# Expert regions over the whole layer, and a reordered preparation, in a macaron block with a routed mixture

## The chip, the cores and the metric

The kernel runs on one core of one Trainium2 chip. The metric is the device time of one execution in microseconds (us); the profiled execution is a run of its own. Engines: PE (TensorE, matrix products; PEld its weight loads), DVE (VectorE), ACT (ScalarE), POOL (GpSimd), SP (SyncE, which here only issues DMAs); "SPq" is an engine's sequencer.

## The reference

x is 2 x 2048 tokens of 256 numbers. Three residual steps follow one another: half a mixture of experts, a linear attention, and half the same mixture again.

```python
def _L0_ffn_ref(h, router_w, rn_g, rn_b, w1, ln_g, ln_b, w2, on_g, on_b):   # 4 experts, hidden 512
    h_norm = layer_norm(h, rn_g, rn_b)
    g = softmax(einsum('bsd,ed->bse', h_norm, router_w))
    top2_w, top2_idx = top_k(g, 2)
    top2_w = top2_w / (sum(top2_w) + EPS_GATE)
    hid = relu(layer_norm(einsum('bsd,edh->bseh', h, w1), ln_g, ln_b))
    expert_out = einsum('bseh,ehd->bsed', hid, w2)
    out = sum(take_along_axis(expert_out, top2_idx) * top2_w)
    return layer_norm(out, on_g, on_b)
x = x + 0.5 * _L0_ffn_ref(_layernorm(x), ...)
x = x + _L0_attn_ref(_layernorm(x), ...)     # Z = cumsum(v k^T), y = q Z, 16 heads of 16
x = x + 0.5 * _L0_ffn_ref(_layernorm(x), ...)
```

## The kernel before

**Tiles.** The 4096 tokens are 32 token tiles of 128 (`NT`); 16 of them make a group (`GT`), 8 an octet (`TO`), 4 a quad (`TB`). A mixture takes the groups G = 0, 1 (first mixture, f = 0) and 2, 3 (second, f = 1). For each group the tokens are routed: normalised (`quad_norm`, `quad_rstd`, `quad_factors`, `quad_again`), written as two f16 parts (`row` on ACT, `row_low` on DVE), turned (`row_T`), multiplied by the router (`router`), and for each octet `logits`, `exps`, `choose`, `prefix` and `place` find the two experts of every token and its row in an expert's region of the DRAM tensor `slots_in`. POOL's `scatter` then writes each token tile twice (two indirect DMAs). Each region is closed by rows of zeros (`pads`, SP). `tables` works out, from the counts, which expert (`etab`) and which row (`rtab`) each *slot tile* of 256 rows belongs to. With 4 experts, a group's 4096 slots fill at most `NJ` = 16 + 3 = 19 slot tiles, so a mixture runs `NP` = 38, the kernel 76.

**A slot tile.** SP loads its rows (`load_slots`: two transposing DMAs into `hT`, one plain into `hs`; 5 buffers of `hT`, 3 of `hs`) up to `AHEAD` = 5 slot tiles ahead. On PE: `grams` (variance of the hidden row by the Gram matrix of w1), `std_T`, `layer1` in two halves, `layer2` of the slot tile before in two halves. DVE: `twice_low`, `variances`, `std_parts`, `relu_low`; POOL: `pair_std` (the power -1/2 of the variance, L613); ACT: `std_row`, `relu_high`, `scale_out`. SP stores the scaled result (`store_slots`) to `slots_out`. PE runs `grams` two slot tiles ahead, so slot tile j + 2's load has to have landed when slot tile j begins.

**Order.** Each engine's queue is written out by hand in a function `mixture(f)` of its own; an engine does its queue in order, and semaphores are the only links. SP's queue at slot tile p is: store p - 1, then load p + 5. At the first load of a group (J = 0) it first writes that group's pads and waits until all 16 token tiles of the group are scattered and `tables` is done; whatever stands behind it in SP's queue, stores included, waits too.

**Beside the slot tiles** of a mixture's first group (J = 0 to 18) the second group is routed: `ROUTED` spreads the 16 token tiles over J = 0 to 9, `OCTET_AT` = (5, 10) says where an octet's logits stand, `moves` where POOL scatters it: two token tiles each at J = 7 to 10 and 12 to 15. `tables` stands at J = 12. At J = 14 to 17 DVE adds an offset to X, and in the first mixture `ahead` scales the attention's weights there (`attention_maxima`, `max_row(3)`, `attention_scales`). Beside the second group's slot tiles (from J = 1 on) the first group's results are gathered, weighted and normalised, one token tile per slot tile (`gather`, `first_weighted`, `token_sum`, `token_out`). The second group's results leave during the attention (f = 0) or at the end (`gather_last`, f = 1).

**Preparation**, before the first slot tile, in the `weights` functions: the first group is routed whole, w1 is centred (`centre`), turned (`w1_T`) and multiplied into 4 Gram matrices (`w1_gram`, 16 f32 matmuls each; Gram e waits for `gram_low(e - 2)` on DVE), the scale of w1 is found (`hidden_scales`), gamma is multiplied in (`with_gamma`), w1 is cut in two f16 parts (`w1_high`, `w1_low`), the scale of w2 is found (`output_scale`) and w2 is cut too (`w2_high`, `w2_low`). `layer2` reads w2's parts; in the second mixture they are loaded back from `w2_kept`, since the attention keeps rows in their place.

## Time and profile before

| | us |
|---|---|
| median of 3 runs (1130.91 to 1135.23) | 1131.0 |
| the profiled execution, whole | 1138.73 |
| its span, first to last instruction | 1137.0 |

In the profiled execution the first `layer1` matmul (L1893) starts at 133.8 us; slot tiles 0 to 37 (first mixture) run to about 426, the attention to about 786, slot tiles 38 to 75 to 1072, and the rest gathers and normalises the last group. Slot tile j of the second mixture is number 38 + j. A slot tile has 8 matmuls of line L1893, which makes that line a clock for the others.

### The profile page before, as it was taken

The numbers are of one execution on the slowest core, as the hardware profiler recorded it, in microseconds if no ns is written. First come the engines' busy times: TensorE is split into PE (matmuls) and PEld (weight loads), VectorE is DVE, ScalarE is ACT, GpSimd is POOL, SyncE is SP. The second block draws the span as 40 slices with busy tenths as digits, with TensorE's granted clock in tenths as the row PEclk, the third lists the DMA queues.
The fourth block names the chain that finished last, engine by engine and source line by source line (L and its number), as shares of the span: only waits on it lengthen the run. The fifth ranks groups of instructions, "written<-read, shape, count | busy, mean of one in ns | idle before, by whom it ended". The sixth has DMA issues, their size and how long they took to land.

```text
span 1137.0 us, 26666 instructions
## 1 busy us (share of the span) xinstructions
PE 872.4 (77%) x8596; PEld 662.4 (58%) x8596; DVE 732.4 (64%) x2104; ACT 500.6 (44%) x958; POOL 561.3 (49%) x631
## 2 busy tenths in 40 slices
PE   1543499978999897798788787775799989999700
PEld 1432387856888774565555554443687778888500
DVE  4547776666777754598787764372675774878335
ACT  2642366422444454565565555430565333444311
POOL 4146224551456453687685366354226542555373
PEclk9956599999999998999899899995899999999955
DMA  8042654563566411111121112123645657666343
GB/s 296 10 158 111 157 155 127 152 168 106 130 158 163 130 63 24 40 40 46 43 51 46 23 44 68 31 77 107 159 103 158 155 154 155 163 159 151 118 131 107
DMA packets 191146, 126.06 MB, mean 111 GB/s; under 512 B 126373, under 2 KB 180905, under 8 KB 190633
## 3 DMA queue, kind: packets, MB, share of 16 engines
q1 hardware_dynamic: 177746, 89.72, 30.1%
q0 software_dynamic: 12288, 33.57, 10.1%
q8 instruction: 79, 1.29, 0.5%
q10 hardware_dynamic: 984, 1.07, 0.3%
q14 instruction: 49, 0.40, 0.1%
HBM read 50.89 MB, written 47.19 MB: 86 GB/s over the span
## 4 chain that ended last, share of the span: by engine, by line
PE 48%; DVE 14%; issue 13%; POOL 7%; ACT 6%; DMA 5%; SPq 3%; another core or an unknown queue 3%; ACTq 0%; DVEq 0%; POOLq 0%
PE banks L1908 4%; PE banks L1895 4%; PE banks L1893 4%; PE banks L1894 4%; PE banks L1910 4%; PE banks L1909 4%; PE banks L1993 4%; POOL slots_in L605 3%; PE banks L1995 3%; PE banks L2106 3%; PE banks L1994 3%; PE banks L1869 2%; PE banks L1870 2%; DMA area<-slots_out,pos 2%
## 5 line engine op out<-in xcount | busy, mean ns | idle before, releaser
L613 POOL TENSOR_TENSOR stds<-vare,expo 128x4 f32<-128x4 f32 x76 | 80.5, 1059 | 208.3 <-DVE vare L920 207.0
L1908 PE MATMUL banks<-w2all,area 128*128 x608 | 167.0, 275 | 6.3 <-DMA w2all<-w_kept 3.6
L1893 PE MATMUL banks<-area,w1h 128*128 128x256 f16 x608 | 169.1, 278 | 2.1 <-DVE area L934 1.9
L1895 PE MATMUL banks<-area,w1l 128*128 128x256 f16 x608 | 168.5, 277 | 0.9 <-issue 0.9
L1894 PE MATMUL banks<-area,w1h 128*128 128x256 f16 x608 | 168.9, 278 | 0.3 <-issue 0.2
L1910 PE MATMUL banks<-w2all,area 128*128 x608 | 166.7, 274 | 1.8 <-issue 1.8
L1909 PE MATMUL banks<-w2all,area 128*128 x608 | 166.7, 274 | 0.0
L934 DVE SCALAR_TENSOR_TENSOR area<-banks,area 128x512 f16<-128x512 f32 x152 | 104.4, 687 | 88.2 <-ACT area L1451 75.2
L1451 ACT ACTIVATE area<-banks 128x512 f16<-128x512 f32 x152 | 89.6, 590 | 123.8 <-PE banks L1895 99.8
L605 POOL DMA_INDIRECT slots_in<-area,spos x96 | 102.9, 1072 | 75.4 <-DVE spos L855 49.6
L737 POOL TENSOR_TENSOR area<-area 128x512 f16<-128x512 f32 x64 | 79.3, 1244 | 119.0 <-ACT area L1663 118.4
L1459 ACT ACTIVATE area<-banks,stds 128x256 f32<-128x256 f32 x152 | 70.9, 466 | 98.6 <-PE banks L1910 80.3
L629 POOL DMA_INDIRECT area<-slots_out,pos x96 | 97.0, 1010 | 25.8 <-issue 21.6
L1993 PE MATMUL banks<-area 64*128 64x32 f16 (+1 forms) x766 | 76.6, 226 | 41.5 <-issue 21.5
L1869 PE MATMUL banks<-gramh,area 128*128 x304 | 77.9, 290 | 24.9 <-issue 11.0
L1993 PEld LDWEIGHTS banks<-area 64*128 64x128 f16 (+1 forms) x766 | 39.9, 96 | 77.7 <-issue 51.0
L915 DVE CUSTOM_DVE_ANT_0 area<-banks,area 128x256 f16<-128x256 f32 x152 | 58.3, 420 | 33.0 <-PE banks L1870 27.2
L1995 PE MATMUL banks<-area 64*128 64x32 f16 (+1 forms) x766 | 75.9, 221 | 4.5 <-issue 4.5
L1870 PE MATMUL banks<-graml,area 128*128 x304 | 77.9, 291 | 0.6 <-issue 0.6
L1994 PE MATMUL banks<-area 64*128 64x32 f16 (+1 forms) x766 | 75.5, 222 | 2.2 <-issue 2.2
L1663 ACT ACTIVATE area<-area 128x512 f16<-128x512 f32 x64 | 40.1, 628 | 71.1 <-DVE area L1325 68.4
L1908 PEld LDWEIGHTS banks<-w2all,area 128*128 128x128 f16 x608 | 59.5, 98 | 19.5 <-issue 7.5
(278 smaller groups left out, 2226.3 us busy)
## 6 DMA issues: line engine op xcount, KB each, us to landing
area<-slots_in SPq DMA_DIRECT2D x76, 256.0 KB
slots_out<-area SPq DMA_DIRECT2D x152, 128.0 KB
X<-in_L_attn_x_dram SPq DMA_DIRECT2D x8, 512.0 KB, 6.1
slots_in<-zrow SPq DMA_DIRECT2D x16, 256.0 KB
area<-area SPq DMA_DIRECT2D x256, 16.0 KB
out_dram<-X SPq DMA_DIRECT2D x32, 128.0 KB
area<-slots_in SPq DMA_TRANSPOSE x152
area<-in_L_ffn_w_dram SPq DMA_DIRECT2D x4, 512.0 KB, 11.7
```

Source lines behind the costliest of these rows:

```text
L605: pool.indirect_dma_start(slots_in[G % 2], bass.IndirectOffsetOnAxis(spos[:, O % 2, k, j:j + 1], 0), rows_of(i).rearrange("p c d -> p (c d ...
L934: dve.scalar_tensor_tensor(out=Rl[:, p % 2, ms].rearrange("p m t -> p (m t)"), in0=bank[k][:, :], scalar=0.0, in1=Rh[:, p % 2, ms].rearran ...
L1869: pe.matmul(o, a[:, c], gramh[c][:, bass.ds(e, 1), :], start=(c == 0), stop=False)
L1893: pe.matmul(o, w1h[c][m][:, bass.ds(e, 1), :], a[:, c], start=(c == 0), stop=False)
L1894: pe.matmul(o, w1h[c][m][:, bass.ds(e, 1), :], a[:, KC + c], start=False, stop=False)
L1895: last = pe.matmul(o, w1l[c][m][:, bass.ds(e, 1), :], a[:, c], start=False, stop=(c == KC - 1))
L1908: pe.matmul(o, Rh[:, p % 2, k, rows], w2h[k][:, bass.ds(e, 1), :], start=(k == 0), stop=False)
L1909: pe.matmul(o, Rh[:, p % 2, k, rows], w2l[k][:, bass.ds(e, 1), :], start=False, stop=False)
L1910: last = pe.matmul(o, Rl[:, p % 2, k, rows], w2h[k][:, bass.ds(e, 1), :], start=False, stop=(k == HC - 1))
L1993: pe.matmul(o, lh, rh, start=start, stop=False, **kw)
L1994: pe.matmul(o, lh, rl, start=False, stop=False, **kw)
L1995: return pe.matmul(o, ll, rh, start=False, stop=stop, **kw)
```

## The change

1. An expert's region now holds a whole mixture, 32 token tiles, and the counts run on over both groups (`carry` isn't cleared between them). So a mixture's slot tiles are `NP` = 32 + 3 = 35, and the kernel's 70. `slots_in` and `slots_out` are one tensor each.
2. As not all tokens are routed when the first slot tiles run, `tables` is done in three phases (`PHASE` = 0, 5, 13): slot tiles 0 to 4 need octet 0 alone, 5 to 12 the whole first group, 13 to 34 everything. SP waits for octets and table at slot tiles 0, 5 and 13. `positions` has to map a row through these segments. Its rows are longer than before.
3. The second group is routed sooner: token tiles over j = -1 to 4, logits at j = 2 and 5, POOL's scatters 3, 3 and 2 token tiles at j = 4, 5, 6 and again at 7, 8, 9; pads at j = 9, the last table at j = 8. Loads of slot tiles 13 and up are issued 4 ahead, and none before j = 10 (`load_at`). The first group leaves from j = 20 on by `LEFT`, one or two token tiles per slot tile, 13 slot tiles in all.
4. In the preparation the Grams stand sooner in the queues of PE, ACT and DVE, the first table right behind octet 0, both quads' statistics of the next group before the first slot tile, and w2's low parts behind the first slot tiles' variances. The last 4 token tiles of the first group are scattered between POOL's first `pair_std`. `std_T(p + 1)` now stands ahead of `layer1(p)` on PE.
5. In the attention two tables are worked out (phases 0 and 1 of the second mixture) instead of one, and SP's first five loads of the second mixture wait for octet 0 alone; the reload of w2 waits for both octets.

The diff, cut to its core:

```diff
-    REG = GT * P + S2
+    NO = NT // TO
+    NP = NT + E - 1
+    SPARE = NT * P + S2
+    REG = SPARE + (E - 1) * S2
+    PHASE = (0, TO - E + 1, GT - E + 1, NP)
+    SEGS = (1, 3, 4)
+    NB = SEGS[-1] * E
+    K1 = GT + E - 1
     AHEAD = 5
...
+
+        ROUTED = (0, 3, 6, 8, 11, 14, 16)
+        OCTET_AT = (2, 5)
+        MOVED = (3, 3, 2)
+        LEFT = (2, 1, 1, 2, 1, 1, 2, 1, 1, 1, 1, 1, 1)
+        LAST_AT = 10
         OFFSET_AT = 14
 
+
+        def started(j):
+            return ROUTED[max(0, min(j + 2, len(ROUTED) - 1))]
+
         def routed(j):
-            return tuple(range(ROUTED[j], ROUTED[j + 1])) if j + 1 < len(ROUTED) else ()
+            return range(started(j - 1), started(j))
 
 
         def moves(j):
             for o, at in enumerate(OCTET_AT):
-                if at + 2 <= j < at + 2 + TO // 2:
-                    t = TO * o + 2 * (j - at - 2)
-                    return t, t + 1
+                k = j - at - 2
+                if 0 <= k < len(MOVED):
+                    return range(TO * o + sum(MOVED[:k]), TO * o + sum(MOVED[:k + 1]))
             return ()
...
+        def leaves(j):
+            k = j - K1 - 1
+            return range(sum(LEFT[:k]), sum(LEFT[:k + 1])) if 0 <= k < len(LEFT) else ()
+
...
             def load_slots(p):
-                G, J = group(p)
-                if J == 0:
-                    pads(G)
+                f, j = p // NP, p % NP
+                if j in PHASE:
+                    sp.wait_ge(r_tab, 3 * f + PHASE.index(j) + 1)
+                if j == PHASE[0]:
+                    sp.wait_ge(sc_h[0], 32 * TO * (2 * f + 1))
+                if j == PHASE[1]:
+                    sp.wait_ge(sc_h[1], 32 * TO * (2 * f + 1))
+                if j == PHASE[2]:
                     for o in range(GO):
-                        sp.wait_ge(sc_h[o], 32 * TO * (G + 1))
-                    sp.wait_ge(sc_p[G % 2], 16 * E * (G // 2 + 1))
-                    sp.wait_ge(r_tab, G + 1)
-                row = sp.value_load(rtab[0:1, G % 2, J:J + 1], min_val=0, max_val=(E - 1) * REG + GT * P - S2)
+                        sp.wait_ge(sc_h[o], 32 * TO * (2 * f + 2))
+                    sp.wait_ge(sc_p, 16 * E * (f + 1) + 16)
+                row = sp.value_load(rtab[0:1, j:j + 1], min_val=0, max_val=E * REG - S2)
                 wait(sp, b_A, 2 * (p - R_HT + 1))
                 for k in range(2):
...
+            def load_at(j):
+                return j - AHEAD if j < PHASE[2] else max(j - AHEAD, LAST_AT, j - 4)
...
+                    for o in range(GO):
+                        sp.wait_ge(sc_h[o], 32 * TO * 3)
                     sp.wait_ge(m_w2, 16)
                     sp.dma_start(w2flat, w2_kept).then_inc(m_w2, 16)
-                for p in range(p0, p1):
-                    if p > p0:
-                        store_slots(p - 1, 0)
-                        store_slots(p - 1, 1)
-                    if p + AHEAD < p1:
-                        load_slots(p + AHEAD)
-                store_slots(p1 - 1, 0)
-                store_slots(p1 - 1, 1)
+                for j in range(NP):
+                    if j > 0:
+                        store_slots(p0 + j - 1)
+                    if j == LAST_AT - 1:
+                        pads(f)
+                    for i in range(NP):
+                        if load_at(i) == j:
+                            load_slots(p0 + i)
+                store_slots(p1 - 1)
...
-                for t in range(GT):
+                for t in range(GT - TB):
...
+                Q1 = GQ * (G + 1)
+                quad_rstd(Q1)
                 pair_std(p0)
+                if f == 0:
+                    scatter(GT - 4)
+                    scatter(GT - 3)
+                quad_rstd(Q1 + 1)
                 pair_std(p0 + 1)
-                for p in range(p0, p0 + NP):
-                    g, j = group(p)
-                    if g == G and j % 2 == 0 and j // 2 < GQ:
-                        quad_again(GQ * (G + 1) + j // 2)
-                    moved = moves(j) if g == G else ()
-                    for t in moved[:1]:
+                if f == 0:
+                    scatter(GT - 2)
+                    scatter(GT - 1)
+                for j in range(NP):
+                    p = p0 + j
+                    if j < GQ:
+                        quad_again(Q1 + j)
+                    if j + 2 < NP:
+                        pair_std(p + 2)
+                    if j + 2 < GQ:
+                        quad_rstd(Q1 + j + 2)
+                    for t in moves(j):
                         scatter(GT * (G + 1) + t)
```

The tables and the two orders on DVE and PE (of long pieces a few lines stand):

```diff
+            def tables(f, phase):
+                lo, hi = PHASE[phase], PHASE[phase + 1]
+                nb = SEGS[phase] * E
+                last = phase == len(SEGS) - 1
+                step(dve.tensor_tensor(cnt[:, :], carry[:, :], regbase[:, :], ALU.subtract))
+                if last:
+                    dve.tensor_copy(padp[:, :], carry[:, :]).then_inc(r_pad, 1)
+                up = {0: ((1, -1),), 1: ((2, -1), (3, 1)), 2: ((4, 1),)}[phase]
+                for row, sign in up:
+                    ins = dve.tensor_scalar(bound[:, E * row:E * row + E], cnt[:, :], 1.0 / S2, sign * (S2 - 1) / 2 / S2,
+                                            ALU.mult, ALU.add)
+                step(ins)
+                new = bound[:, E * up[0][0]:E * up[-1][0] + E]
+                step(dve.tensor_scalar(new, new, ROUND, None, ALU.add))
+                step(dve.tensor_scalar(new, new, ROUND, None, ALU.subtract))
...
+                if f > 0 and phase == 0:
+                    for r in range(R_Y):
+                        dve.wait_ge(st_y[r], 16 * uses(2 * NP, r, R_Y))
+                dve.tensor_copy(rtab[:, lo:hi], row)
+                step(dve.tensor_scalar(row, row, 1.0 / REG, -(REG - 1) / 2 / REG, ALU.mult, ALU.add))
+                step(dve.tensor_scalar(row, row, ROUND, None, ALU.add))
+                step(dve.tensor_scalar(row, row, ROUND, None, ALU.subtract))
+                dve.tensor_copy(etab[:, lo:hi], row).then_inc(r_tab, 1)
...
+                hidden_maxima()
+                tables(0, 0)
+                max_row(1)
+                row_lows(12, 14)
                 hidden_scales()
-                row_lows(12, 16)
-                chain(1)
-                tables(0)
+                row_lows(14, 16)
+                gram_low(0)
+                gram_low(1)
                 with_gamma(0)
+                logits(1)
                 with_gamma(1)
-                gram_low(0)
+                choose(1)
                 with_gamma(2)
-                gram_low(1)
+                place(1)
                 with_gamma(3)
+                output_maxima()
                 gram_low(2)
+                quad_norm(GQ)
                 gram_low(3)
-                for c in range(KC):
-                    for m in range(HC):
-                        w1_low(c, m)
-                output_scale()
-                for k in range(HC):
-                    w2_low(k)
-                dve.wait_ge(l_on, 32)
-                dve.tensor_scalar(ong[:, :], ong[:, :], 0.5, None, ALU.mult)
-                dve.tensor_scalar(onb[:, :], onb[:, :], 0.5, None, ALU.mult).then_inc(p_on, 1)
-                dve.wait_ge(p_on, 1)
+                for m in range(HC):
+                    w1_low(0, m)
+                max_row(2)
+                for m in range(HC):
+                    w1_low(1, m)
+                quad_norm(GQ + 1)
...
                 w1_T(2)
+                w1_gram(1)
                 tokens(10, 12)
+                w1_T(3)
                 maxima_T(1)
                 maxima_all(1)
                 tokens(12, 16)
-                w1_gram(1)
+                w1_gram(2)
                 prefix(1)
-                w1_T(3)
-                w1_gram(2)
                 w1_gram(3)
                 maxima_T(2)
                 maxima_all(2)
...
                         grams(p + 2, e[p + 2])
+                    if j + 1 < NP:
+                        std_T(p + 1, i1 + started(j - 2))
                     layer1(p, 0, e[p])
...
+                    for t in turn[:1]:
+                        pe.wait_ge(b_sdr, p + 2)
+                        row_T(i1 + t)
+                    if j > 0:
                         layer2(p - 1, 0, e[p - 1])
-                    if here and octet(j, 1) is not None:
+                    for t in turn[1:2]:
+                        row_T(i1 + t)
+                    layer1(p, 1, e[p])
+                    for t in turn[2:]:
+                        row_T(i1 + t)
+                    if j > 0:
+                        layer2(p - 1, 1, e[p - 1])
+                    if octet(j, 1) is not None:
                         prefix(O1 + octet(j, 1))
```

**Three places in the queues.** DVE (VectorE), the end of the preparation, of before: Gram parts (L1064), w1's low parts (L1071), the maximum and the scale of w2 (L1082 to L1089), w2's low parts (L1076), then the statistics of the next quad.

```order
L1054 TENSOR_TENSOR area<-area 128x1024 [waits p_gam,p_wt]
...
L1064 SCALAR_TENSOR_TENSOR graml<-banks,sc,gramh 128x256 [waits p_gh]
...
L1071 TENSOR_TENSOR w1l<-area,w1h 128x512 [waits p_w1h] x8
L1082 TENSOR_REDUCE mxw<-area 128x1 [waits l_w2]
...
L992 TENSOR_TENSOR q<-q,capn 128x1 [waits dve_done]
...
L1089 TENSOR_SCALAR sc<-sc,qi 128x1 [waits dve_done]
L1076 SCALAR_TENSOR_TENSOR w2all<-area,q,w2all 128x1024 [waits p_w2h] x4
L1134 TENSOR_SCALAR ong<-ong 128x256 [waits l_on]
...
L782 BN_STATS xst<-X 128x6 [waits r_rows_high,l_x4,p_on]
```

The same place now: L1150 are the Gram parts, L1140 the gamma product, L840 the logits of octet 1, L1163 the maximum of w2, L1157 w1's low parts, L973 the first slot tile's `twice_low`.

```order
L1150 SCALAR_TENSOR_TENSOR graml<-banks,sc,gramh 128x256 [waits p_gh]
...
L1140 TENSOR_TENSOR area<-area 128x1024 [waits p_gam,p_wt]
...
L840 SCALAR_TENSOR_TENSOR lga<-banks,qi,r 128x32 [waits r_rstd_again,r_logits_psum]
...
L1163 TENSOR_REDUCE mxw<-area 128x1 [waits l_w2]
...
L1150 SCALAR_TENSOR_TENSOR graml<-banks,sc,gramh 128x256 [waits p_gh]
...
L815 BN_STATS xst<-X 128x6 [waits r_rows_high,l_x4]
...
L1157 TENSOR_TENSOR w1l<-area,w1h 128x512 [waits p_w1h] x4
...
L815 BN_STATS xst<-X 128x6 [waits r_rows_high,l_x5]
...
L973 SCALAR_TENSOR_TENSOR area<-area 128x512 [waits l_slots0]
```

The first two Gram parts moved ahead of gamma and of octet 1's routing, the maximum of w2 into the wait for the third, both quads' statistics ahead of the scale of w2, and w2's low parts out of this piece altogether.

POOL (GpSimd), the second octet's scatters beside the first group's slot tiles, of before; L605 is one indirect DMA (two to a token tile), L613 the `pair_std` for the slot tile two ahead.

```order
L605 DMA slots_in<-area,spos 9216x512 [waits r_rows_low,r_slots_found]
L605 DMA slots_in<-area,spos 9216x512
L613 TENSOR_TENSOR stds<-vare,expo 128x4 [waits b_out_scaled,b_var_guarded]
L605 DMA slots_in<-area,spos 9216x512 x4
L613 TENSOR_TENSOR stds<-vare,expo 128x4 [waits b_out_scaled,b_var_guarded]
L605 DMA slots_in<-area,spos 9216x512 x4
L613 TENSOR_TENSOR stds<-vare,expo 128x4 [waits b_out_scaled,b_var_guarded]
L605 DMA slots_in<-area,spos 9216x512 x4
L613 TENSOR_TENSOR stds<-vare,expo 128x4 [waits b_out_scaled,b_var_guarded]
L605 DMA slots_in<-area,spos 9216x512 x2
```

And now (L635 the scatter, L642 `pair_std`):

```order
L642 TENSOR_TENSOR stds<-vare,expo 128x4 [waits b_out_scaled,b_var_guarded]
L635 DMA slots_in<-area,spos 20480x512 [waits r_rows_low,r_slots_found]
L635 DMA slots_in<-area,spos 20480x512 x5
L642 TENSOR_TENSOR stds<-vare,expo 128x4 [waits b_out_scaled,b_var_guarded]
L635 DMA slots_in<-area,spos 20480x512 x6
L642 TENSOR_TENSOR stds<-vare,expo 128x4 [waits b_out_scaled,b_var_guarded]
L635 DMA slots_in<-area,spos 20480x512 x4
```

Where 4 stood between two `pair_std` there are 6, 6 and 4; the octet takes three slot tiles, j = 7 to 9, where it took four, J = 12 to 15.

SP (SyncE) at the first slot tile whose table needs the second group, of before (L480 stores of slot tile 13, L451 and L452 pads, L463 the first read of the new table, for slot tile 19):

```order
L480 DMA slots_out<-area 128x256 [waits b_out_scaled] x2
L451 TENSOR_LOAD padp [waits r_pads_found]
...
L452 DMA slots_in<-zrow 128x2x512
...
L463 TENSOR_LOAD rtab [waits pads_written1,r_tables,scattered1,scattered0]
...
L466 DMA_TRANSPOSE area<-slots_in 128x4x128
...
L469 DMA area<-slots_in 128x2x512 [waits b_h2]
L480 DMA slots_out<-area 128x256 [waits b_out_scaled] x2
```

And now (L503 stores, of slot tiles 7 and 8, later 9; L470 and L471 pads; L486 for slot tile 13):

```order
L503 DMA slots_out<-area 128x256 [waits b_out_scaled] x4
L470 TENSOR_LOAD padp [waits r_pads_found]
...
L471 DMA slots_in<-zrow 128x2x512
...
L503 DMA slots_out<-area 128x256 [waits b_out_scaled] x2
L486 TENSOR_LOAD rtab [waits scattered1,pads_written,scattered0,r_tables]
...
L489 DMA_TRANSPOSE area<-slots_in 128x4x128
...
L492 DMA area<-slots_in 128x2x512 [waits b_h2]
...
L503 DMA slots_out<-area 128x256 [waits b_out_scaled] x2
```

The read that waits for everything stood 5 slot tiles ahead of the slot tile that needs it (at 14 for 19); now it stands 3 ahead (at 10 for 13), behind the store of slot tile 9, and the pads stand one slot tile before it.

## Rows read from the trace of the kernel before

**Rows 1.** Windows, line L1893 alone: length, PE and PEld busy (matmuls), clock, DMA share, GB/s.

```profile
133.70:171.60 37.90, 11.62 (x40) 4.09 (x41) 0.95 0.64 171
171.60:210.90 39.30, 10.90 (x40) 3.86 (x40) 1.00 0.50 133
210.90:240.90 30.00, 8.72 (x32) 3.23 (x33) 0.98 0.69 163
240.90:283.80 42.90, 9.76 (x32) 3.42 (x32) 0.89 0.44 128
...
795.90:879.20 83.30, 22.81 (x80) 8.12 (x80) 0.96 0.53 135
879.20:907.40 28.20, 8.72 (x32) 3.08 (x33) 1.00 0.69 173
907.40:939.50 32.10, 9.09 (x32) 3.25 (x33) 0.95 0.50 157
939.50:1057.70 118.20, 39.26 (x144) 14.09 (x145) 1.00 0.63 152
```

**Rows 2.** Windows, busy time (instructions) of each engine in the preparation.

```profile
59.30:118.80 59.50, 22.42 (x127) 17.83 (x127) 37.21 (x104) 18.46 (x36) 29.28 (x27) 0.61 0.39 137
```

**Rows 3.** Timeline of PE in the preparation: start, us, line, operation [idle before <- who ended it].

```profile
94.37 6.92 PE L1750 MATMUL banks<-area 128*128 128x256 f32 x18 [8.34 <-DVE graml L1064]
```

**Rows 4.** Timeline of DVE in the preparation.

```profile
86.55 0.15 DVE L860 TENSOR_TENSOR padf<-carry,regbase 128x4 f32<-128x4 f32 x1
...
89.98 0.40 DVE L879 CAST rtab<-choice 128x19 int32<-128x19 f32 x1
...
101.76 0.88 DVE L1064 SCALAR_TENSOR_TENSOR graml<-banks,sc,gramh 128x256 f16<-128x256 f32 x2 [3.48 <-ACT gramh L1502]
105.22 0.88 DVE L1064 SCALAR_TENSOR_TENSOR graml<-banks,sc,gramh 128x256 f16<-128x256 f32 x2 [2.58 <-ACT gramh L1502]
...
120.05 4.87 DVE L1076 SCALAR_TENSOR_TENSOR w2all<-area,q,w2all 128x1024 f16<-128x1024 f32 x4 [1.22 <-ACT w2all L1512]
...
125.36 1.41 DVE L782 BATCH_NORM_STATS2 xst<-X 128x6 f32<-128x256 f32 x4
...
134.69 0.29 DVE L886 TENSOR_TENSOR choice<-choice 128x128 f32<-128x128 f32 x1
```

**Rows 5.** Timeline of POOL beside slot tiles 13 to 17.

```profile
236.67 1.04 POOL L613 TENSOR_TENSOR stds<-vare,expo 128x4 f32<-128x4 f32 x1
...
239.24 0.96 POOL L605 DMA_INDIRECT slots_in<-area,spos  x1 [0.30 <-issue]
```

**Rows 6.** Timeline of POOL, a scatter of octet 1 in the preparation.

```profile
94.07 2.12 POOL L605 DMA_INDIRECT slots_in<-area,spos  x1 [0.30 <-issue]
```

**Rows 7.** Timeline of PE, the first layer2 of the second mixture.

```profile
809.89 0.30 PE L1908 MATMUL banks<-w2all,area 128*128 x1 [3.62 <-DMA w2all<-w_kept]
```

**Rows 8.** Timeline of PE, Gram 68 and the start of slot tile 66.

```profile
1005.53 0.27 PE L1869 MATMUL banks<-gramh,area 128*128 x1
...
1006.41 0.27 PE L1893 MATMUL banks<-area,w1h 128*128 128x256 f16 x1
```

**Rows 9.** Timeline of SP, the load for slot tile 71.

```profile
1014.62 2.57 SPq L466 DMA_TRANSPOSE area<-slots_in  x2
```

**Rows 10.** Timeline of SP, the group boundary of the second mixture.

```profile
927.78 2.72 SPq L466 DMA_TRANSPOSE area<-slots_in  x2
```

**Rows 11.** Timeline of PE, the Gram that this load feeds.

```profile
932.12 0.28 PE L1869 MATMUL banks<-gramh,area 128*128 x1 [1.18 <-DMA area<-slots_in]
```

**Rows 12.** Timeline of SP at the group boundary, first mixture.

```profile
263.75 2.55 SPq L466 DMA_TRANSPOSE area<-slots_in  x2
```

**Rows 13.** Waits of PE from 228 to 285 us: us in total, times, longest.

```profile
PE banks L1762 <- issue: 3.9, 1, 3.9
...
PE banks L1987 <- DVE bvB L1283: 2.7, 1, 2.7
```

**Rows 14.** Timeline of ACT at the end of the attention.

```profile
781.84 0.95 ACT L1673 ACTIVATE area<-banks,sc 64x256 f32<-64x256 f32 x2 [13.07 <-remote]
```

509 lines of the change are left out of this document (259 added, 250 removed).

## The prediction

> **What bounds the kernel now.** I read the windows first. Line L1893 has 8 matmuls per slot tile, so its count says how many slot tiles a window holds: 38 start between 133.7 and some 426 us, 38 more between 795.9 and 1072. Where nothing else happens, 18 slot tiles take 118.2 us, 6.57 each, with the granted clock at 1.00, that is 2.4 GHz [rows 1]. That is TensorE (PE) without a pause; I call it the pace. Other windows are the pace plus holes: at the first group's start 37.9 us for 5 slot tiles; at the group boundary of the first mixture 42.9 us for 4 at clock 0.89, of the second 32.1 for 4 at 0.95 [rows 1]. The first 133.7 us, the preparation, are another bound: in 59.5 us of it VectorE (DVE) is busy 37.2, PE 22.4 at clock 0.61 [rows 2], and PE stands 8.34 us until DVE delivers the low part of a Gram [rows 3]. It is a chain through DVE, ACT and PE in which each waits for another. The attention, 796 less 414, is hardly touched.
>
> The profiled execution lasts 1138.73 us (span 1137.0), 0.7% over the median. I work out a difference in the trace's microseconds and take it from 1131.0 as it stands; 0.7% of 40 us is nothing.
>
> **Fewer slot tiles.** 35 instead of 38 per mixture: 3 x 6.57 = 19.7 us less in each, as the steady window costs no more per slot tile than PE needs [rows 1]. The tokens' work beside them stays; gathers are squeezed into 13 slot tiles instead of 16, on POOL and DVE, which in the steady part are not the bound. **-39.4 us.**
>
> **Preparation, 133.7 us.** The scale of w2 is done at 118.8. The stretch to it holds 59.5 - 37.2 = 22.3 us in which DVE idles [rows 2]. Two of these idle times, 3.48 and 2.58 us, are waits for Gram parts [rows 4]; with the Grams sooner in all three queues and the maximum of w2 put into the wait, I let both go, and half of the 8.34 us before PE's Gram 2 [rows 3]: 6.06 + 4.17 = 10.2 us. Two quads' statistics now stand ahead of that scale, 1.41 us of BN_STATS each [rows 4] and a little more, say 1.9 (one of them stood behind it before). Bounds: nothing gained and both added, +3.8; all 22.3 gained less those, -18.5. I stand in the middle, at -10.2, since the table, some 3.8 us from 86.55 to its last cast at 89.98 + 0.40 [rows 4], stays in this stretch and DVE can't be filled whole. From there to the first layer1 are 14.9 us. Out of them go 4.87 and the 1.22 in front for w2's low parts [rows 4], 6.1 in all. Into them come two token tiles' scatters before pair_std of slot tile 1: 4 indirect DMAs at 0.96 + 0.30 [rows 5] = 5.0, of which I let 2 lie beside work; std_T(1) now stands ahead of layer1(0), so the other 3 count. Net -3.1. **-13.3** (-22 to +4; the three token tiles routed just before slot tile 0 are in the upper end).
>
> DVE's gamma product and POOL meet here: one scatter took 2.12 us where others took 0.96 [rows 5, 6]. The Trainium skill, "SBUF — State Buffer", section "Who interferes with whom", has it that a DVE instruction with two SBUF inputs shuts GpSimd's reads out until it ends; w2's low parts are such instructions and now fall beside scatters and the first pair_std. The trace agrees for that row; by the rule the preparation would be some 4 x 1.16 = 4.6 us longer than my sum. My sum leaves it out, since the scatters of [rows 5] have other DVE work beside them and stay at 0.96.
>
> **Slot tiles 0 to 4, first mixture (37.9 us).** They take over what left the preparation. Before, slot tiles 5 to 9 with 8 token tiles took 39.3 us, so a token tile costs (39.3 - 5 x 6.57)/8 = 0.8 us [rows 1]. Now 13 token tiles stand in slot tiles 0 to 4 instead of 8: 5 x 0.8 = 4.0. DVE does w2's low parts there, 4.87, and positions through three segments instead of one, some 7 operations more at 0.29 [rows 4], 2.0. All of it in series would be 10.9; were PE the only bound, 5.5 (6.57 x 5 + 13 x 0.8 = 43.4). In slot tile 0 and 1 DVE is clearly over the pace with all this, and PE waits for its variances and relu parts, so I stand near the upper end. **+9.6** (+5 to +14). Nearly all that moving w2 gives comes back here.
>
> **Slot tiles 5 to 9 (39.3).** Routing is done by j = 4. What remains are scatters: 6, 6 and 4 indirect DMAs per slot tile, 6 x 1.26 + 1.04 for pair_std = 8.6 us of POOL against a pace of 6.57 [rows 5]. POOL falls some 4 us behind in two slot tiles, and pair_std waits in its queue; it runs two slot tiles ahead, which covers most. 5 x 6.8 + 3 = 37. **-2.3** (-6 to +6). The second mixture's slot tiles 0 to 9 (83.3) lose the 3.62 us wait for w2's reload [rows 7], since ahead of it in SP's queue now stand five loads that need octet 0 alone, and the scatters it waits for are over before the first layer2; **-3.8**.
>
> **Slot tiles 10 to 13, a new wait.** The load for 13 is issued at j = 10 behind the store of slot tile 9. A store and the load behind it stand late in a slot tile: load 71 is issued 1014.62 - 1006.41 = 8.2 us after slot tile 66 starts [rows 8, 9]. From issue to its Gram are 932.12 - 927.78 = 4.3 us [rows 10, 11]. A Gram two slot tiles ahead stands 1006.41 - 1005.53 = 0.9 us before the start of a slot tile [rows 8], so Gram 13 so long before slot tile 11. So PE waits 8.2 + 4.3 - (6.57 - 0.9) = 6.8 us. Window: 4 x 6.57 + 6.8 = 33.1 against 30.0 and 28.2 [rows 1]: **+3.1 and +4.9**. Queued behind that wait on SP are the store of 10 and load 14; 14 still lands in time. Bounds: no wait (-6.8) if PE is late already; +4 if POOL's last scatter ends after the store.
>
> **Slot tiles 14 to 17 (42.9 and 32.1).** The old boundary goes, where load 19 was issued only at 263.75 [rows 12], over 20 us into the window. What stays in the first mixture are the attention's scales, 3.9 and 2.7 us of PE's waits [rows 13], and 4 x 6.57 = 26.3; with 5 for the rest at low clock, 38, **-4.9**. The second: 30, **-2.1**.
>
> **Thin loads.** From 13 on a load is 4 ahead, not 5: two slot tiles minus 0.9 must hold 8.2 + L, where L is the latency. At L = 4.3 the period is (8.2 + 4.3 + 0.9)/2 = 6.70 against 6.57, over 44 slot tiles (22 per mixture) **+6**. Bounds: 0, at L = 4.0; at 5.5, 7.3 and +32.
>
> **Attention.** Two tables and longer positions on DVE, 4 to 7 us, part beside POOL's scatters; loads issued sooner. **+3** (0 to 7).
>
> Sum: -39.4 - 13.3 + 9.6 - 2.3 - 3.8 + 3.1 + 4.9 - 4.9 - 2.1 + 6 + 3 = **-39.2**; 1131.0 - 39.2 = **1092**.
>
> **Rivals.** *Boundary covered:* PE is a little late by j = 10, so load 13 costs nothing, and the thin loads neither. Speaks for it that POOL and ACT hold PE up in j = 7 to 9 anyway. -13.6 (twice 6.8) - 6: **1072**. Chance 0.20.
>
> *Hold-ups in the denser scatters:* at the end of the attention ACT stood 13.07 us, released by nothing on the core, while POOL scattered the last octet [rows 14]. The clock of 0.89 at the boundary [rows 1] shows that PE paused there too. With 16 scatters in three slot tiles instead of four, twice per mixture, one such hold-up less 3 us of lead would cost 10 us more per mixture: 1092 + 20 = **1112**. Chance 0.20. Against it: the indirect DMAs themselves took 0.96 throughout. The Trainium skill, "DMA: Bandwidth & Descriptors", section "Queues, rings and completion order", says that each DMA engine goes round robin between queues packet by packet, so scatters and loads share 16 engines; no row here separates that from a wait for memory.
>
> *Starved loads, slower:* in the same formula all that is gained (1131 - 1092 + 6 = 45) is eaten when each of 44 slot tiles loses 1.03 us, that is from L = 2 x 7.60 - 9.1 = 6.1 us on. At L = 6.7 the period is 7.9, + 58: 1131 - 45 + 58 = **1144**. For it: the DMA share is 0.63 with 13 slot tiles of gathers now denser [rows 1], and L was measured at the boundary, where SP had stood still and few transfers ran. Against: PE never waits for a load in 118.2 us of steady work, though that has a slot tile more of lead. Chance 0.05.
>
> *Does it do what it says?* The 35 slot tiles are a plain count, so no. What can fail is the preparation: no gain there, +10: 1102, within the range. Chance 0.07 for it and the like.
>
> **How the numbers follow.** Forecast 0.48, covered 0.20, hold-ups 0.20, starved 0.05, others 0.07. Range 1068 to 1118: from the covered case less a little more of the preparation, to the hold-ups plus part of the load bound; left out are starving and half of the others. A measurement of this kernel can tell about 0.5%, 5.7 us. Faster 0.91, within 0.5% 0.04 (loads at L = 6), slower 0.05.
>
> **What would show it.** First layer1 near 120 us; slot tiles 0 to 4 above 45 us with DVE busy all through; a wait of 5 to 8 us of PE for the load (released by DMA) before Gram 13 and in the second mixture the same; the steady slot tiles at 6.57 to 6.7 with small DMA waits in each; no wait at the old boundary; attention 382 to 388 us. If steady slot tiles stand at 6.57 and Gram 13 doesn't wait, the covered case holds; if PE's Gram waits exceed 1 us in every slot tile, the starved one. If the preparation stays above 128, my reading of DVE's idle time was wrong.

## The result, and the profile after

The changed kernel is **slower**: 1162.1 us against 1133.1, a ratio of 1.0235 with a 95% interval of 1.0177 to 1.0292; when it ran again later, beside 1133.0, 1165.5 and 1.0284 (1.0216 to 1.0351). 1092 was forecast, 1068 to 1118. Its profiled execution spans 1161.2 us against 1137.0, 24.2 more, with 6 slot tiles fewer.

The windows of line L1997, the first matmul of layer1 (8 per slot tile; the windows end where a slot tile starts), in the changed kernel; columns as in [rows 1]: length, PE and PEld busy (matmuls), granted clock, DMA share, GB/s.

```profile
126.10:180.40 54.30, 12.62 (x40) 4.39 (x40) 0.85 0.45 125
180.40:231.20 50.80, 13.02 (x40) 4.58 (x40) 0.79 0.45 130
231.20:267.30 36.10, 9.36 (x33) 3.33 (x33) 0.86 0.44 121
267.30:307.00 39.70, 9.07 (x33) 3.25 (x33) 0.91 0.32 83
307.00:444.00 137.00, 38.73 (x136) 13.69 (x136) 0.94 0.45 119
...
811.30:906.80 95.50, 23.77 (x81) 8.40 (x81) 0.92 0.46 131
906.80:940.80 34.00, 8.82 (x32) 3.12 (x32) 0.90 0.44 128
940.80:967.50 26.70, 8.80 (x33) 3.15 (x33) 1.00 0.52 120
967.50:1097.00 129.50, 38.51 (x136) 13.66 (x136) 0.96 0.51 127
```

The stages beside those of [rows 1] (what has no row there is the distance of the same marks in the trace of before; a mixture's end is its last `layer2` matmul and some 1 us, 426.0 and 444.0, 1073.0 and 1097.0):

| stage, us | before | after | measured | forecast |
|---|---|---|---|---|
| preparation | 133.7 | 126.1 | -7.6 | -13.3 |
| slot tiles 0 to 4, first mixture | 37.9 | 54.3 | **+16.4** | +9.6 |
| 5 to 9 | 39.3 | 50.8 | **+11.5** | -2.3 |
| 10 to 13 | 30.0 | 36.1 | +6.1 | +3.1 |
| 14 to 17 | 42.9 | 39.7 | -3.2 | -4.9 |
| 18 to the end | 142.2 | 137.0 | **-5.2** | -16.7 |
| attention | 369.9 | 367.3 | -2.6 | +3 |
| 0 to 9, second mixture | 83.3 | 95.5 | **+12.2** | -3.8 |
| 10 to 13 | 28.2 | 34.0 | +5.8 | +4.9 |
| 14 to 17 | 32.1 | 26.7 | -5.4 | -2.1 |
| 18 to the end | 133.5 | 129.5 | **-4.0** | -16.7 |
| last group's results | 64.0 | 64.2 | +0.2 | 0 |
| sum | | | +24.2 | -39.2 |

("18 to the end" has three slot tiles fewer and half of the thin loads' +6 in its forecast.) Of the 63 us between forecast and measurement, 37 lie in slot tiles 0 to 9, 24 from slot tile 18 on, 6 in the preparation; the other stages take 3 or 4 back. In the first two places the granted clock is lower than it was: 0.85, 0.79 and 0.92 against 0.95, 1.00 and 0.96 in slot tiles 0 to 9, 0.94 and 0.96 against 0.99 and 1.00 from 18 on. A clock is either 1.2 or 2.4 GHz, so 0.79 over the 50.8 us of slot tiles 5 to 9 means (1 - 0.79) x 2 = 42% of the time, 21 us, at 1.2 GHz, in which PE did half of what it does at 2.4. That is at most 11 us lost by the clock (less where PE would have waited anyway), about what that stage grew by.

What a stretch of it looks like, on PE alone, in the changed kernel; columns: length, PE busy (matmuls), clock, DMA share, GB/s.

```profile
204.00:208.00 4.00, 4.00 (x39) 1.00 0.46 137
208.00:212.00 4.00, 4.00 (x39) 1.00 0.81 169
212.00:216.00 4.00, 1.48 (x9) 0.87 0.48 163
216.00:220.00 4.00, 3.60 (x17) 0.50 0.36 128
220.00:224.00 4.00, 2.76 (x12) 0.50 0.28 101
224.00:228.00 4.00, 4.00 (x20) 0.50 0.20 64
```

39 matmuls in 4 us at full clock; then, from 212 on, 9 of them; then, from 215.0 on, the clock is at 0.50 for 13.7 us, and even where PE is busy all through it does 20. POOL's timeline beside it:

```profile
206.50 1.04 POOL L635 DMA_INDIRECT slots_in<-area,spos  x1 [0.20 <-issue]
...
213.87 1.04 POOL L642 TENSOR_TENSOR stds<-vare,expo 128x4 f32<-128x4 f32 x1
215.11 1.25 POOL L635 DMA_INDIRECT slots_in<-area,spos  x1 [0.20 <-issue]
...
221.73 0.96 POOL L635 DMA_INDIRECT slots_in<-area,spos  x1 [0.30 <-issue]
```

These are the first of the 6 indirect DMAs of slot tile 7, the pair_std for 9, and the first and the last of the 6 of slot tile 8: 12 indirect DMAs from 206.5 to 222.7 with nothing between them but one pair_std.

### The profile page after: what moved, and what is told of

It reads as the page before. It is cut to its first block, busy times and chain, and to the rows that moved or that the text cites. A ratio compares the mean times of both kernels' runs of the same rounds, so it can differ in the third digit from the quotient of the medians.

```text
span 1161.2 us, 25520 instructions
## 1 busy us (share of the span) xinstructions
PE 860.9 (74%) x8236; PEld 643.2 (55%) x8236; DVE 735.6 (63%) x2108; ACT 493.1 (42%) x928; POOL 548.1 (47%) x625
## 4 chain that ended last, share of the span: by engine, by line
PE 39%; DVE 19%; issue 13%; DMA 7%; ACT 7%; POOL 6%; SPq 4%; another core or an unknown queue 4%; DVEq 0%; ACTq 0%; POOLq 0%
PE banks L2095 3%; PE banks L1997 3%; DMA area<-slots_out,pos 3%; PE banks L1999 3%; PE banks L1998 3%; PE banks L2014 3%; PE banks L2012 3%; PE banks L2013 3%; PE banks L2097 3%; PE banks L2096 3%; DMA area<-slots_in 2%; PE banks L2208 2%; PE banks L1973 2%; POOL area L659 2%
## 5 line engine op out<-in xcount | busy, mean ns | idle before, releaser
L642 POOL TENSOR_TENSOR stds<-vare,expo 128x4 f32<-128x4 f32 x70 | 72.7, 1038 | 282.6 <-DVE vare L987 282.5
L1001 DVE SCALAR_TENSOR_TENSOR area<-banks,area 128x512 f16<-128x512 f32 x140 | 96.3, 688 | 115.1 <-ACT area L1551 91.1
L1997 PE MATMUL banks<-area,w1h 128*128 128x256 f16 x560 | 162.7, 291 | 2.4 <-issue 2.4
L1998 PE MATMUL banks<-area,w1h 128*128 128x256 f16 x560 | 162.7, 290 | 1.5 <-issue 1.4
L1999 PE MATMUL banks<-area,w1l 128*128 128x256 f16 x560 | 162.5, 290 | 1.1 <-issue 1.1
L2012 PE MATMUL banks<-w2all,area 128*128 x560 | 156.2, 279 | 1.8 <-issue 1.5
L2013 PE MATMUL banks<-w2all,area 128*128 x560 | 155.7, 278 | 0.8 <-issue 0.8
L2014 PE MATMUL banks<-w2all,area 128*128 x560 | 155.3, 277 | 1.1 <-issue 1.1
L770 POOL TENSOR_TENSOR area<-area 128x512 f16<-128x512 f32 x64 | 79.7, 1254 | 112.9 <-ACT area L1768 110.1
L635 POOL DMA_INDIRECT slots_in<-area,spos x96 | 96.4, 1004 | 76.7 <-DVE spos L885 49.2
L1551 ACT ACTIVATE area<-banks 128x512 f16<-128x512 f32 x140 | 82.6, 590 | 102.0 <-PE banks L1999 87.3
L1559 ACT ACTIVATE area<-banks,stds 128x256 f32<-128x256 f32 x140 | 65.6, 468 | 104.5 <-PE banks L2014 70.0
L2095 PE MATMUL banks<-area 64*128 64x32 f16 (+1 forms) x766 | 75.0, 223 | 39.7 <-issue 21.0
L2095 PEld LDWEIGHTS banks<-area 64*128 64x128 f16 (+1 forms) x766 | 39.7, 96 | 71.5 <-issue 44.5
L1974 PE MATMUL banks<-graml,area 128*128 x280 | 77.2, 306 | 2.5 <-issue 2.5
L1544 ACT ACTIVATE area<-banks 1x512 f16<-1x512 f16 x70 | 40.5, 579 | 87.0 <-PE banks L1985 68.0
L1997 PEld LDWEIGHTS banks<-area,w1h 128*128 x560 | 57.6, 103 | 19.7 <-issue 5.2
## 6 DMA issues: line engine op xcount, KB each, us to landing
area<-in_L_ffn_w_dram SPq DMA_DIRECT2D x4, 512.0 KB, 11.5
```

The source lines that it names most:

```text
L635: pool.indirect_dma_start(slots_in, bass.IndirectOffsetOnAxis(spos[:, O % 2, k, j:j + 1], 0), rows_of(i).rearrange("p c d -> p (c d)"), No ...
L1997: pe.matmul(o, w1h[c][m][:, bass.ds(e, 1), :], a[:, c], start=(c == 0), stop=False)
L1998: pe.matmul(o, w1h[c][m][:, bass.ds(e, 1), :], a[:, KC + c], start=False, stop=False)
L1999: last = pe.matmul(o, w1l[c][m][:, bass.ds(e, 1), :], a[:, c], start=False, stop=(c == KC - 1))
L2012: pe.matmul(o, Rh[:, p % 2, k, rows], w2h[k][:, bass.ds(e, 1), :], start=(k == 0), stop=False)
L2013: pe.matmul(o, Rh[:, p % 2, k, rows], w2l[k][:, bass.ds(e, 1), :], start=False, stop=False)
```

## The experiments

Ratios are against the kernel before on the same chip. Each group of runs has a chip's own value of the kernel before (1133 to 1141 us), so differences between groups are read in ratios and in the lengths of stages. "Unexplained" below is the sum of the distances between two starts on PE that are over 0.3 us apart and for which the profile names no releaser, from the first indirect DMA of a run to 3 us behind the last. A run ends where POOL issues no indirect DMA for over 2.5 us. "The end" of the slot tiles in the experiments is 5.7 us after the last `layer1` starts, in every kernel; by that mark slot tiles 18 to the end take 136.3 and 129.6 us before, 131.6 and 125.5 in the changed kernel, and 129.8 and 122.9 when the changed kernel ran again, so differences under some 3 us in one such stage say little.

### 1. Do dense scatters alone do it?

The kernel before with 3, 3 and 2 token tiles, and nothing else:

```diff
-                if at + 2 <= j < at + 2 + TO // 2:
-                    t = TO * o + 2 * (j - at - 2)
-                    return t, t + 1
+                k = j - at - 2
+                if 0 <= k < len(MOVED):          # MOVED = (3, 3, 2)
+                    return tuple(range(TO * o + sum(MOVED[:k]), TO * o + sum(MOVED[:k + 1])))
```

> The kernel before, and POOL scatters an octet as 3, 3 and 2 token tiles in three slot tiles instead of two in each of four; nothing else. Theory C (the denser scatters as such hold PE up at slot tiles 4 to 9 of the changed kernel): slower than the kernel before by 10 us or more, with slot tiles of 10 to 14 us at J = 7 to 9. Rival D (the density of the routing, three token tiles in one slot tile on ACT, DVE and PE, and not of the scatters): within 3 us of the kernel before.

Measured: ratio 1.0213 (1.0177 to 1.0249), 1165.8 us against 1140.6. Theory C holds, and at one spot that is larger than it said. Windows of slot tiles 6 to 9, line L1894, which is the first matmul of layer1 here:

```profile
180.90:188.40 7.50, 2.18 (x9) 0.78 (x8) 1.00 0.43 104
188.40:196.50 8.10, 2.21 (x9) 0.78 (x8) 1.00 0.58 158
196.50:213.40 16.90, 2.69 (x8) 1.00 (x8) 0.71 0.40 128
213.40:221.80 8.40, 2.36 (x9) 0.78 (x8) 0.98 0.47 141
```

Slot tile 8 takes 16.9 us instead of 7.5 (17.3 instead of 8.3 in the second mixture), slot tile 7, with as many scatters, 8.1. The same place on PE alone:

```profile
190.00:194.00 4.00, 4.00 (x47) 1.00 0.62 131
194.00:198.00 4.00, 3.23 (x33) 1.00 0.68 221
198.00:202.00 4.00, 1.91 (x23) 1.00 0.79 214
202.00:206.00 4.00, 3.16 (x15) 0.68 0.25 94
206.00:210.00 4.00, 2.50 (x12) 0.50 0.24 98
210.00:214.00 4.00, 3.78 (x21) 0.54 0.26 97
```

and single matmuls of it:

```profile
198.83 0.27 PE L1909 MATMUL banks<-w2all,area 128*128 x1
...
200.70 0.27 PE L1911 MATMUL banks<-w2all,area 128*128 x1 [1.17 <-issue]
201.42 0.27 PE L1909 MATMUL banks<-w2all,area 128*128 x1 [0.45 <-issue]
202.14 0.27 PE L1910 MATMUL banks<-w2all,area 128*128 x1 [0.45 <-issue]
```

PE does one or two matmuls every 0.7 or 1.4 us (it needs 0.11 at full clock), waits for nothing that the trace shows, and 4 us after the first such gap (199.3) the clock halves, at 203.4. POOL's scatters run on at their 0.96 us each. The kernel before has a short piece of this at its slot tile 13 and a long one at the end of the attention, which [rows 14] shows as ACT's 13.07 us with a releaser outside the core. There the trace of before holds no matmul in the last 5.6 us of it; the run of section 5 with pair_std first has that wait with its releaser, PE, whose matmuls come mostly 0.7 and 1.4 us apart up to 794.8:

```profile
795.08 0.95 ACT L1779 ACTIVATE area<-banks,sc 64x256 f32<-64x256 f32 x2 [12.58 <-PE banks L2098]
```

The same kernel with octet 0 spread over J = 7, 9 and 11, so that the slot tiles between are free of scatters; octet 1 stays dense:

```diff
+        MOVED = ((3, 0, 3, 0, 2), (3, 3, 2))
```

> The kernel before with octet 0 scattered as 3, 0, 3, 0 and 2 token tiles at J = 7 to 11, octet 1 as 3, 3 and 2 at J = 12 to 14. In the run with 3, 3, 2 for both, slot tile 8 took 17.0 and 17.3 us instead of 7.5 and 8.3, slot tile 7 8.1 as before. Theory G (two full slot tiles in a row are needed: 12 indirect DMAs without a pause): J = 7 to 11 all under 9 us, and so in all about 18 us faster than that run, if not for octet 1. Rival H (six in one slot tile are enough): J = 9 takes 12 us or more.

Measured: 1.0054 (1.0031 to 1.0077). Slot tiles 7 to 10, line L1895:

```profile
191.20:198.90 7.70, 2.18 (x8) 0.78 (x8) 1.00 0.56 161
198.90:206.60 7.70, 2.19 (x9) 0.79 (x9) 1.00 0.59 167
206.60:214.60 8.00, 2.18 (x8) 0.78 (x8) 1.00 0.56 150
214.60:221.50 6.90, 2.22 (x9) 0.78 (x8) 1.00 0.57 155
```

No slot tile over 8.0 (8.2 in the second mixture), clock 1.00; octet 1, dense, has 11.3 and 17.1 us at J = 13 and 14, against 9.5 and 15.2 before (13.9 and 12.0 against 7.3 and 11.1 in the second mixture). Theory G holds for octet 0: the same scatters cost nothing with a pause. Over all runs the unexplained time of PE goes with the length of an unbroken run of scatters and with its pace. In slot tiles, at over 0.7 indirect DMAs per us, runs of 4 have 0 to 2 us, of 6 mostly 2 to 4, of 8 3 to 6, of 12 7 to 12. At 0.6 to 0.7 per us, as the kernel before has at J = 7 to 10, 6 have up to 1.4, 8 have 1.3 and 10 have 1.3 to 5.4. The 16 at the end of the attention, in every kernel, have 10 to 17, with one other instruction of POOL of 2.3 us among them. The clock comes on top. (One run of 4, in the kernel before at J = 14, has 5.4 us; the 3.9 us of L1762 [rows 13] are in it.)

The changed kernel with 4, 0, 4:

```diff
-        MOVED = (3, 3, 2)
+        MOVED = (4, 0, 4)
```

> The changed kernel with octets scattered as 4, 0 and 4 token tiles (j = 4 and 6, and 7 and 9) instead of 3, 3, 2. Theory G (PE comes to a crawl in the second of two slot tiles that POOL fills with scatters; with two in four and a pause no more, as at J = 7 to 11 of the spaced run, 7.7 to 8.0 us): slot tiles 4 to 9 (64.1 and 64.0 us of the changed kernel) some 10 us shorter in each mixture, 20 us faster in all. Rival: 8 indirect DMAs in one slot tile (10.1 us of POOL against 6.5) and 8 more right behind at j = 6 and 7 are the same load again: within 5 us of the changed kernel.

Measured: 1.0394 (1.0325 to 1.0463), the slowest of all. The pause was there, but the runs of 8 before and behind it were themselves long enough for 3 to 6 us of unexplained time each, four times per mixture, and the last one ended so late that slot tile 10 took 19.0 and 17.6 us. So my condition "two full slot tiles in a row" was too narrow: what counts is the unbroken run, and 8 is too long by itself. With 16 token tiles to scatter in the 6 slot tiles that the change leaves, there is no spacing that keeps runs at 4.

### 2. The density of the routing

The kernel before with three token tiles in slot tiles 2, 4 and 6:

```diff
-        ROUTED = (0, 2, 3, 5, 6, 8, 10, 11, 13, 14, 16)
+        ROUTED = (0, 2, 4, 7, 8, 11, 12, 15, 16)
```

> The kernel before with the second group's token tiles routed as 2, 2, 3, 1, 3, 1, 3, 1 over J = 0 to 7 instead of 2, 1, 2, 1, 2, 2, 1, 2, 1, 2 over J = 0 to 9. In the changed kernel slot tile 3, with three token tiles and no scatter, takes 10.0 us in both mixtures at full clock, where two take 7.7. Theory (density of the routing costs by itself): slot tiles 2, 4 and 6 take 9.5 to 10 us, those with one 7.1: 3 x 2.2 less what the emptier ones give back (some 1 each), about 3 to 5 us per mixture, ratio 1.005 to 1.008. Rival (the 10.0 us are from std_T in front of layer1, not from the third token tile): ratio 1.000.

Measured: 1.0068 (1.0027 to 1.0109). Slot tiles 2, 4 and 6 take 9.5, 9.3 and 9.7 us, those with one token tile 7.2. Slot tiles 0 to 9 together 79.9 us against 77.2 in the first mixture, 85.6 against 83.3 in the second: +2.7 and +2.3. The theory holds, a little under its price. The third token tile costs 2 us, not the 0.8 that I had for each; ACT's part is the likely reason, though no run shows it: in slot tile 3 of the changed kernel ACT has 18 operations, busy 8.1 of 10.0 us.

### 3. The preparation and w2

The changed kernel with w2's low parts back ahead of slot tile 0:

```diff
                     output_scale()
+                    for k in range(HC):
+                        w2_low(k)
...
-                if f == 0:
-                    w2_low(0)
-                    w2_low(1)
...
-                    w2_low(2)
-                    w2_low(3)
```

> The changed kernel with w2's four low parts back ahead of the first slot tile. Theory E (moving them gives nothing, DVE is the bound on both sides of the start): first layer1 5 to 6 us later than in the changed kernel (126.1), slot tiles 0 and 1 together 16 to 17 us instead of 23.8, sum of both 1 us shorter: within 3 us of the changed kernel. Rival F (the low parts cost more beside the slot tiles, since PE then stops and runs on at 1.2 GHz): 4 to 8 us faster than the changed kernel.

Measured: 1.0311 (1.0280 to 1.0342), first layer1 at 132.7 us instead of 126.1, slot tiles 0 to 4 52.5 instead of 54.3 (50.1 when the changed kernel ran again). Neither theory: by the windows the move is a gain of 4.8 or 8.8 us, by which run of the changed kernel stands beside it. By the ratios it is 3 or 9 us, and the intervals overlap, so this run alone shows only that the move is no loss. The same move alone, in the kernel before:

```diff
                 variances(p0 + 1)
+                if f == 0:
+                    w2_low(0)
+                    w2_low(1)
                 twice_low(p0 + 2)
                 std_parts(p0 + 1)
+                if f == 0:
+                    w2_low(2)
+                    w2_low(3)
```

> The kernel before with w2's low parts alone moved beside the first slot tiles (two behind the second variances, two behind the second std_parts; h2 and its scratch moved out of w2's place as in the changed kernel). With them put back, the changed kernel lost 0.8 points of its ratio (1.0311 against 1.0235), its first layer1 came 6.6 us later and slot tiles 0 to 4 were only 1.9 us shorter. Theory: the move is worth 4 to 5 us by itself, since PE's first slot tile then runs beside DVE: ratio 0.996. Rival, my forecast's step: slot tiles 0 and 1 take it back, ratio 1.000.

Measured: 0.9967 (0.9936 to 0.9997), first layer1 at 128.1, slot tiles 0 to 4 41.7 instead of 37.9: of 5.7 us, 3.8 come back there. The theory's number holds, at the edge of what can be told (by the windows the gain is 1.9 us, by the ratio 3.7).

The Grams sooner, alone, in the kernel before (orders of PE, ACT and DVE as in the changed kernel, maximum of w2 too):

```diff
                 row_lows(12, 16)
-                chain(1)
-                tables(0)
-                with_gamma(0)
+                gram_low(0)
+                gram_low(1)
+                with_gamma(0)
+                logits(1)
...
+                place(1)
+                tables(0)
                 with_gamma(3)
+                output_maxima()
                 gram_low(2)
```

> The kernel before with that part of the new preparation alone that puts the Grams sooner in the queues of PE, ACT and DVE and the maximum of w2 into the wait for the third; slot tiles, tables, routing and scatters are as before, and w2's low parts stay ahead of the first slot tile. In the changed kernel the scale of w2 was done some 10 us sooner with two quads' statistics ahead. Theory: first layer1 at 125 to 128 us instead of 133.8, 6 to 9 us faster than the kernel before, the first gain that nothing takes back. Rival: octet 1's scatters now end later, the first loads with them, and the first layer1 comes no sooner: within 2 us.

Measured: 1.0029 (1.0000 to 1.0058), first layer1 at 139.0 us (134.9, 136.1 and 138.0 in three other runs with the old preparation, 133.8 in the shown one). The rival holds: w2's low parts started at 117.2 instead of 120.0, but octet 1's last scatter ended at 122.9 instead of 110.1, and DVE waited 6.2 us for the rows of the first slot tile. (The "some 10 us sooner" of the expectation was misread: in the changed kernel the scale of w2 is done at 114.5 instead of 118.8.) In this kernel SP's first load needs both octets; the sooner Grams only pay with a table that needs octet 0 alone, which is the half of the change that whole-layer regions brought.

POOL's second pair_std ahead of the scatters, in the changed kernel:

```diff
-                if f == 0:
-                    scatter(GT - 4)
-                    scatter(GT - 3)
                 quad_rstd(Q1 + 1)
                 pair_std(p0 + 1)
                 if f == 0:
-                    scatter(GT - 2)
-                    scatter(GT - 1)
+                    for t in range(GT - 4, GT):
+                        scatter(t)
```

> The changed kernel with POOL's second pair_std ahead of the last four token tiles' scatters instead of between them. It came 5.1 us after its variances (118.99 to 124.08) behind four indirect DMAs. If the preparation ends on it: first layer1 at 121 to 122 us instead of 126.1, but 8 indirect DMAs then stand before pair_std of slot tile 2. Forecast: 3 to 5 us faster than the changed kernel, ratio 1.020 to 1.025 on this chip; if slot tile 1 takes it back, 1.028.

Measured: 1.0263 (1.0205 to 1.0320), first layer1 at 123.2, slot tile 0 at 15.7 us instead of 14.1. 2.9 us gained and half of it given back, so the 3 to 5 us that were expected don't show; the whole is within what two runs of the changed kernel differ by.

### 4. Behind slot tile 10: pairs of gathers, thin loads, load 13

ACT in slot tile 21 of the changed kernel. L1568 weights a gathered token tile, L1544 is std_row, L1551 relu_high:

```profile
329.61 0.51 ACT L1568 ACTIVATE area<-area,gate 128x256 f32<-128x256 f32 x1 [1.71 <-DMA area<-slots_out,pos]
332.26 0.51 ACT L1568 ACTIVATE area<-area,gate 128x256 f32<-128x256 f32 x1 [2.15 <-DMA area<-slots_out,pos]
332.67 0.57 ACT L1544 ACTIVATE area<-banks 1x512 f16<-1x512 f16 x1
333.15 0.57 ACT L1551 ACTIVATE area<-banks 128x512 f16<-128x512 f32 x1
```

Two gathers are issued in slot tile 20; in ACT's queue both stand ahead of std_row and relu_high, and relu_high comes 5.6 us after the start of the slot tile (327.6) instead of 1.5. So slot tile 21 takes 10.0 us and 22, at clock 0.79, 8.2; 24 and 27 are the same, and in the second mixture too (in 27 of the first mixture the attention's weights stand as well; the kernel before has them at slot tile 30, of 12.1 us). The second one moved behind scale_out:

```diff
-                    for t in leaves(j - 1):
+                    for t in leaves(j - 1)[:1]:
                         first_weighted(i0 + t)
...
                     if j > 0:
                         scale_out(p - 1, 0)
+                    for t in leaves(j - 1)[1:]:
+                        first_weighted(i0 + t)
```

> The changed kernel, and in ACT's queue the second of two gathered token tiles is weighted behind scale_out of the slot tile before, no longer ahead of relu_high. Theory A (from slot tile 20 on ACT stands on the second gather of a pair, PE stops for 3 to 5 us, and its granted clock then falls to 1.2 GHz for a few us more): slot tiles 21, 24 and 27 of each mixture (10.0, 9.8, 14.6 and 9.9, 10.9, 9.3 us) and the ones behind them (8.2, 8.0, 7.1 and 7.9, 7.2, 6.5) come back to about 7, some 10 us per mixture: 20 us faster than the changed kernel, about 1140 us. Rival B (loads issued four ahead are what PE waits for): not over 3 us faster.

Measured: 1.0184 (1.0146 to 1.0223). Slot tiles 18 to the end 128.4 and 117.4 us instead of 131.6 and 125.5: -3.2 and -8.1, 11 us where 20 were expected, and 7 beside the second run of the changed kernel. Theory A holds for the mechanism, with half of its price or less; slot tile 21 is down to 8.3.

The changed kernel with the loads five ahead again:

```diff
-                return j - AHEAD if j < PHASE[2] else max(j - AHEAD, LAST_AT, j - 4)
+                return j - AHEAD if j < PHASE[2] else max(j - AHEAD, LAST_AT)
```

> The changed kernel with loads of slot tiles 14 and up issued five ahead again (13, 14 and 15 all at j = 10). Rival B: the waits for a load in front of a Gram from slot tile 20 on (2.9, 2.9, 1.3 and 0.9 us in the second mixture) go and with them the stretches at 1.2 GHz: 15 to 25 us faster than the changed kernel. Theory A: these waits only follow from ACT's late scale_out, so at most 8 us faster; the 6.4 us wait before Gram 13 stays under both.

Measured: 1.0240 (1.0196 to 1.0283), no faster than the changed kernel; the same stage 128.6 and 121.7, -3.0 and -3.8, or -1.2 and -1.2 beside its second run. Slot tiles 14 to 20 of the second mixture take 45.7 us, 6.5 each, against 46.5 with four ahead, where two of them take 6.8 and 6.9: loads four ahead all but keep up while nothing disturbs. But theory A's half about the loads, that PE's waits for them only follow from ACT's late scale_out, does not hold. The waits of PE behind slot tile 14 of the second mixture (window 940 to 1097: us in total, times, longest), in the changed kernel, with the second gather later, with five ahead, and with both (the run of section 5 with pair_std first):

```profile
PE banks L1973 <- DMA area<-slots_in: 8.0, 4, 2.9
PE banks L1985 <- DVE s L994: 2.6, 2, 1.4
```

```profile
PE banks L1975 <- DMA area<-slots_in: 5.3, 6, 1.8
```

```profile
PE banks L1985 <- DVE s L994: 8.6, 3, 4.5
```

```profile
PE banks L1986 <- DVE s L993: 3.0, 2, 2.2
```

With ACT's order mended PE still waits 5.3 us for loads; with five ahead it waits for none, and for the standard deviations (`s`) instead. Two limits stand one behind the other there, and only both edits together bring the stage to 114.9 us in the second mixture and 124.3 in the first.

Load 13 ahead of the store of slot tile 9, five ahead as well:

```diff
+                    if j == LAST_AT:
+                        load_slots(p0 + PHASE[2])
                     if j > 0:
                         store_slots(p0 + j - 1)
```

> As the run with loads five ahead, and the load of slot tile 13 stands ahead of the store of slot tile 9 in SP's queue. The wait of PE before Gram 13 was 6.4 and 6.5 us, the two slot tiles around it took 14.2 + 8.3 and 14.2 + 6.8 us. If this load is bound by the store ahead of it and a stall costs its own length and as much again at 1.2 GHz, slot tiles 10 and 11 come down to 14 us together: 7 us less per mixture, 14 us faster than the run with loads five ahead. If POOL's last scatter is what it waits for, under 3 us.

In the changed kernel, SP at that place, and the Gram that waits:

```profile
232.06 3.83 SPq L471 DMA_DIRECT2D slots_in<-zrow  x4
235.94 1.59 SPq L503 DMA_DIRECT2D slots_out<-area  x2
238.80 2.56 SPq L489 DMA_TRANSPOSE area<-slots_in  x2
```

```profile
243.07 0.39 PE L1973 MATMUL banks<-gramh,area 128*128 x1 [6.41 <-DMA area<-slots_in]
```

The load is issued 7.6 us after slot tile 10 starts (231.2), its Gram comes 4.3 us later, after a wait of 6.4: the forecast had 8.2, 4.3 and 6.8. Measured with the load ahead: 1.0201 (1.0163 to 1.0240); slot tiles 10 to 13 34.0 and 31.0 us instead of 35.8 and 35.3. 6 us instead of 14, and the rival is wrong too: what the load then waits for are the pads, whose four DMAs (L471) stand ahead of it in SP's queue and have to have landed. Waits of SP in that run, between 226 and 246 us, and the same row in the second mixture:

```profile
SPq L485 <- DMA slots_in<-zrow: 1.7, 1, 1.7
```

POOL's last scatter ends at 230.6 there and the last pad is issued at 233.8, the load at 237.0. So store and pads stand close together as limits. The pads issued sooner were not tried.

### 5. What is left when these are undone together

> The changed kernel with four things undone at once: second gathers weighted later, loads five ahead, load 13 ahead of store 9, w2's low parts back ahead of the first slot tile. Alone the first three came to 1161, 1166 and 1162 us (the third with the second in it) against 1140.6 for the kernel before on their chip, a ratio of 1.018 to 1.024. If the four add up, about 16 us faster than the changed kernel, ratio 1.010. If the dense scatters and routing in slot tiles 3 to 9 hold all that is left, it can't get below a ratio of 1.005, since 35 us go there. If it is one chain of stalls and each only moves, ratio 1.02 again.

Measured: 1.0138 (1.0109 to 1.0167), 11 to 17 us by the two ratios of the changed kernel, so the four do add up. Slot tiles 18 to the end take 123.9 and 114.5 us, 12 and 15 less than in the kernel before, where 17 undisturbed ones take 111.7 (17 x 6.57); the first mixture has the attention's weights at j = 27 on top. 0 to 9 take 98.7 and 96.3, against 77.2 and 83.3 of the kernel before.

> The changed kernel with second gathers weighted later, loads five ahead, load 13 ahead of store 9, w2's low parts left where the change puts them, and scatters as 4, 0, 4. The run with four undone came to a ratio of 1.0138 with w2 moved back, which costs some 0.4 to 0.8 points: 1.008 without it; with the gain that theory G gives the scatters, 0.99 to 0.995. If the pause doesn't help, 1.008.

Measured: 1.0241 (1.0174 to 1.0308). The scatters as 4, 0, 4 cost what the other edits gave.

> The changed kernel with pair_std first, second gathers weighted later, loads five ahead, load 13 ahead of store 9. All that is left of the known costs are the dense scatters and routing in slot tiles 3 to 9. Those with w2 moved back gave 1.0138; w2's move is worth 0.3 to 0.8 points and pair_std's up to 0.4: 1.003 to 1.010. Under 1.003 would mean that the dense slot tiles cost less than the 30 us that I put to them.

Measured: 1.0130 (1.0078 to 1.0183), no better than with w2 put back; slot tiles 0 to 9 108.1 and 94.1 us, 10 to 13 35.6 and 35.7. So all that was undone without going back to fewer scatters per slot tile gives 12 to 17 us, and what is left over the kernel before stands in slot tiles 0 to 13. That the scatters hold it there is read from the windows and from the kernel before with dense scatters; the changed kernel with its old spacing can't be had. The changed kernel once more, for the chip:

> The changed kernel as it is, to have it on one chip with the runs beside it: a ratio of 1.02 to 1.03 to the kernel before.

Measured: 1.0284 (1.0216 to 1.0351).

### 6. A version that beats both

PE's 3.62 us for w2's reload [rows 7] stood in the kernel before in front of a slot tile of 12.5 us. The kernel before with w2's low parts moved, as above, and the reload behind the third load instead of the fifth:

```diff
                 for p in range(p0, p0 + AHEAD):
+                    if f == 1 and p == p0 + 3:
+                        sp.wait_ge(m_w2, 16)
+                        sp.dma_start(w2flat, w2_kept).then_inc(m_w2, 16)
                     load_slots(p)
```

> The kernel before with w2's low parts beside the first slot tiles (alone: ratio 0.9967) and, in the second mixture, w2's reload issued behind the third slot tile's load instead of the fifth. PE waited 3.62 us for it in front of the first layer2, and slot tile 1 of the second mixture takes 12.5 to 14.1 us in every run of this order. If that wait is the cause, it goes, with its stretch at 1.2 GHz: 5 to 7 us more, ratio 0.991. If the reload's 2 MB only delays the loads of slot tiles 3 and 4, ratio 0.997.

Measured: **0.9874** (0.9821 to 0.9926), 1125.1 us against 1139.7: faster than both kernels. SP issues the reload here:

```profile
784.35 0.46 SPq L488 DMA_DIRECT2D w2all<-w_kept  x1
```

against 800.85 in the trace of before, and the second mixture's slot tile 1 takes 7.1 us instead of 12.5, slot tiles 0 to 4 37.4 instead of 43.2; PE has no wait for the reload any more. A wait of 3.6 us had cost 5.4. With the 4 us of w2's low parts that makes some 10 us of the 14.5; the rest is in no window that I can name, and the interval (8 to 20 us) allows for it.

## Why the prediction was wrong, point by point

**Fewer slot tiles: right, but not at 6.57 each.** Where nothing disturbs, slot tiles take 6.5 to 6.9 (46.5 us for 14 to 20 of the second mixture). But the work beside them doesn't shrink with them. The step that failed is the half sentence that gathers squeezed into 13 slot tiles are "not the bound": it looked at DVE and POOL alone, but ACT's queue stands on each gather ahead of relu_high, and loads four ahead have no reserve behind such a stop. From slot tile 18 on both mixtures together were forecast at -33.4 and came to -9.2; with both limits lifted they come to -27.

**Slot tiles 5 to 9: the step with the wrong sign.** It priced the dense scatters by POOL's own time (8.6 us against 6.57, covered by two slot tiles of lead) and came to -2.3. POOL did as it said: pair_std was late by 4.9 us once, and otherwise POOL waited 2.5 to 5.2 us for the variances in front of it. What it did not see is that PE itself slows down during an unbroken run of scatters. The rival "hold-ups in the denser scatters" was this, from the right row [rows 14], at 10 us per mixture; the run that has it alone lost 9.4 us in slot tiles 5 to 9 in each mixture, and 3.3 and 5.0 more at octet 1: 25 in all. Its price was right for one octet; the changed kernel has two dense octets per mixture. In the second mixture's slot tiles 0 to 9 a term was missing besides: its -3.8 is little more than the reload's 3.62 us, while the thirteen token tiles instead of eight and the longer positions, +4.0 and +2.0 in the first mixture by its own rates, stand there too and were put at nothing. The reload's wait did go; the stage grew by 12.2, 9.0 of it in slot tiles 5 to 9.

**The clock was in one term only** (the 5 us of slot tiles 14 to 17). Every other stall was priced at its length. Load 13 waited 6.4 us, and slot tiles 10 and 11 took 14.2 + 8.3, 9.4 over the pace; in the second mixture it waited 6.5 and they took 14.2 + 6.8, 7.9 over it. The reload's 3.6 us cost 5.4. In all, from the changed kernel's windows, (1 - clock) x length over its slot tiles is 52 us, against 14 in the same sum over the trace of before. These 38 us are the most that the clock can have cost, and they lie inside the stages already told and aren't added to them. The rows had it: 42.9 us for 4 slot tiles at 0.89.

**Slot tiles 0 to 4, +9.6 against +16.4.** The third token tile cost 2 us each (three times, 6 us), not 0.8, and the first dense scatters already begin at j = 4 (13.3 us instead of 7.8, but 8.9 when the changed kernel ran again). Slot tile 0 took 14.1 us instead of 8.3, and 11.9 with w2's parts put back; what holds the other 3.6 no run separates. That w2's low parts would nearly all come back here was wrong in the other direction: the move is worth 2 to 4 us in the kernel before.

**Preparation, -13.3 against -7.6.** From the scale of w2 (done at 114.5) to the first layer1 it is 11.6 us, where the sum had 11.8 (14.9 - 3.1), with the term that I had weighed, POOL's scatters in front of the second pair_std, visible:

```profile
116.24 1.01 POOL L642 TENSOR_TENSOR stds<-vare,expo 128x4 f32<-128x4 f32 x1 [7.70 <-DVE vare L987]
117.43 1.04 POOL L635 DMA_INDIRECT slots_in<-area,spos  x1 [0.17 <-issue]
...
121.54 1.50 POOL L635 DMA_INDIRECT slots_in<-area,spos  x1 [0.30 <-issue]
...
124.08 1.00 POOL L642 TENSOR_TENSOR stds<-vare,expo 128x4 f32<-128x4 f32 x1
```

```profile
114.27 0.21 DVE L1066 TENSOR_SCALAR sc<-sc,qi 128x1 f32<-128x1 f32 x1
...
118.99 0.23 DVE L987 TENSOR_SCALAR vare<-var,sc 128x2 f32<-128x2 f32 x1
```

The variances of slot tile 1 are there at 119.2, its pair_std starts at 124.08. The failed term is the first: the scale was done at 114.5, 4.3 us sooner, not 10.2. Part of that is a slip in the sum: -10.2 is the gain alone, and the 3.8 us of the two quads' statistics, which stand in its bounds, were never taken off it; with them it is -6.4. The first two Gram parts did come 9 us sooner and PE's last Gram 7, but DVE then had the maximum of w2 (4.46 us) ahead of the third part, which ended at 103.1 instead of 102.6. The idle time was real; the work put into it was work that DVE had to do anyway, and without a gap from 88 to 114 us DVE became the bound.

The rule of the Trainium skill, "SBUF — State Buffer", section "Who interferes with whom", that I had set beside the scatters would have made them 4.6 us longer. The trace has one of the four at 1.20 us beside DVE's w2 parts and one at 1.50 beside the `twice_low` behind them (L973, at 121.52), not at 2.12: some 0.8 us in all.

**Load 13: the wait and its size came out** (6.4 and 6.5 us for 6.8), but the size in part by luck: the 8.2 us from the start of a slot tile to the load were read where no pads stand ahead of it, and here 3.8 us of pads, which had no term, are in the 7.6. The pads' landing also holds the load when the store is out of its way. The old boundary went as said. The attention came to -2.6 for +3, which says little: from the last `layer1` of the first mixture to the first of the second the kernel before takes 381.5 us and its version with dense scatters, which has the same attention, 386.9. **The thin loads** cost nothing where nothing disturbs, but behind a late gather PE waits for them: beside the runs with the second gather later, five ahead gives 3 to 4 us in each mixture from slot tile 18 on, about the +6 of the forecast, at other places than it said. The slower rival was the wrong one: four or five ahead alone makes no difference that the ratios show.

**What stays open** is why PE crawls in a run of scatters. No semaphore is involved, DMA share falls during it (0.79, then 0.25), which speaks against plain bandwidth; PE's instructions come at multiples of 0.7 us. Nor does the trace show the loading of instructions by DMA: the changed kernel has no transfer of that kind between 209.5 and 225 us, where PE crawls, and the one in the run with dense scatters (203.1, 1.0 us long, as others are) comes 4 us after the crawl began. The rule of the Trainium skill that I had set beside this rival ("DMA: Bandwidth & Descriptors", "Queues, rings and completion order": DMA engines go round robin between queues) doesn't explain it by these rows: PE waits for no transfer while it crawls, and no run here shows the rule at work. Whether it is how PE's instructions reach it, or something that the descriptors of indirect DMAs occupy, no run here separates; a version with the same rows written by other DMAs wasn't tried. The split of slot tiles 0 to 4 between routing and scatters is from single windows, not from a run.

## What to carry to other kernels

Price a stall of the tensor engine of 3 us or more above its length, for the clock behind it (3.6 us cost 5.4, 6.4 cost 9.4, 6.5 cost 7.9), and look at the granted clock of the windows that a change will fill more densely. Work "beside" the critical engine isn't free because its own engine has time: ask what stands behind it in an in-order queue (a gather in ACT's), and whether it comes in a burst. When one of two edits gives nothing, see whether the wait has only changed its name, and try both together. Removing 8% of the main loop's steps can cost more than it gives, if it forces the remaining side work into fewer of them.

## What the runs showed of the hardware

- During unbroken runs of indirect DMAs from GpSimd, one per 1.3 us, TensorE's matmuls come 0.7 and 1.4 us apart, though the profile names nothing that it waits for: mostly 2 to 4 us in a run of 6, 3 to 6 in one of 8, 7 to 12 in one of 12, 10 to 17 in one of 16, up to 2 in runs of 4. At 0.6 to 0.7 per us it is less: up to 1.4 in runs of 6. The cause is open.
- TensorE needn't stop for its clock to fall: one or two matmuls every 0.7 to 1.4 us, for some 3 or 4 us, were followed by 1.2 GHz (granted clock 0.50) for 10.2 and 13.7 us.
- SP's transposing load takes 4.3 us from issue to the matmul that uses it, at the boundary and in the changed kernel alike. SP issues four pads' DMAs 1.1 to 1.2 us apart, and each lands 2.2 us after its issue.
